# Memory attention: a slot's base as the bias of eight exponentials, and pauses in the written order

## The reference, cut to what matters

```python
q = _ln((x @ Wq.T + bq).reshape(-1, 48, 16), gq, bq_ln)
scores = jnp.einsum('bnd,nkd->bnk', q, key)              # 64 keys per slot
_, topi = jax.lax.top_k(flat, 8)
mask = jnp.ones_like(flat).at[..., topi].set(0.0)
sc = softmax(flat + -1000000.0 * mask)                   # over the eight kept
out = (einsum('bnk,nkd->bnd', sc, value) + q @ Wres.T + bres) @ Wmem.T + bmem
```

## Time and profile before

| | before |
|---|---|
| median of 3 runs | 4503.36 us (4493.08 to 4503.57) |
| profiled execution | 4485.82 us, span 4484.5 us |
| instructions | 52962 |
| TensorE busy, whole span | 3254.5 us (73%) |
| VectorE | 2467.1 us (55%) |
| ScalarE | 1627.5 us (36%) |
| GpSimd | 1403.0 us (31%) |
| memory attention | from the start to about 765 us |

### The profile page before, as it was taken

How to read it: one execution, slowest core, us unless ns; L and a number is a source line. 1 busy time by engine, 2 the same in 40 slices (tenths; PEclk the granted TensorE clock), 3 DMA queues, 4 the chain that set the end, 5 groups by cost and what they waited for, 6 DMA issues and landing times. The chain is left out here.

```text
span 4484.5 us, 52962 instructions
## 1 busy us (share of the span) xinstructions
PE 3254.5 (73%) x17693; PEld 2099.2 (47%) x17693; DVE 2467.1 (55%) x6511; ACT 1627.5 (36%) x3647; POOL 1403.0 (31%) x1086
## 2 busy tenths in 40 slices
PE   5988886868906666666888888467689567667698
PEld 3666665646602222223566656245456323235455
DVE  6878774364337788885323323545442277765443
ACT  3666653111205444542333333324212244434311
POOL 3666664104352434452212211200010244430010
PEclk7888888879958889898999999679769788889889
DMA  2000001203440000000000000110111200000000
GB/s 88 5 8 8 6 8 39 92 19 102 115 137 0 0 0 0 0 0 14 7 1 1 1 1 1 37 77 1 65 51 28 71 0 0 0 26 1 1 1 19
DMA packets 71034, 116.12 MB, mean 26 GB/s; under 512 B 28689, under 2 KB 58537, under 8 KB 68018
## 3 DMA queue, kind: packets, MB, share of 16 engines
q1 hardware_dynamic: 61170, 86.50, 5.7%
q0 software_dynamic: 9600, 26.23, 2.3%
HBM read 88.58 MB, written 24.12 MB: 25 GB/s over the span
## 5 line engine op out<-in xcount | busy, mean ns | idle before, releaser
L1223 POOL TENSOR_TENSOR L_attn_state<-L_attn_state,L_attn_ccol 128x1024 f32<-128x1024 f32 x192 | 451.7, 2353 | 589.3 <-DVE L_attn_state L1216 586.6
L1216 DVE TENSOR_TENSOR_SCAN L_attn_state<-L_attn_decay,bank 128x1024 f32<-128x1024 f32 x192 | 438.3, 2283 | 25.0 <-PE bank L1182 10.4
L1182 PE MATMUL bank<-L_attn_state,ident 128*128 128x512 f32 x768 | 408.1, 661 | 28.6 <-POOL L_attn_state L1223 28.6
L1176 PE MATMUL bank<-L_attn_parts,L_attn_select 96*128 96x512 bf16 x384 | 133.7, 432 | 257.5 <-DVE bank L1208 246.1
L1193 ACT ACTIVATE L_attn_decay<-L_attn_dt,L_attn_A 128x512 f32<-128x512 f32 x384 | 256.1, 715 | 142.9 <-DVE L_attn_state L1216 139.5
L1102 POOL TENSOR_TENSOR L_xattn_prob<-L_xattn_prob,L_xattn_inv 128x1024 f32<-128x1024 f32 x64 | 121.1, 1893 | 567.0 <-DVE L_xattn_inv L1085 567.0
L1208 DVE TENSOR_TENSOR bank<-L_attn_dtx,bank 128x1024 f32<-128x1024 f32 x192 | 235.9, 1229 | 72.2 <-PE bank L1176 66.4
L1182 PEld LDWEIGHTS bank<-L_attn_state,ident 128*128 128x128 f32 x768 | 161.2, 212 | 190.9 <-issue 122.8
L1198 ACT COPY L_attn_ccol<-bank 128x512 f32<-128x512 f32 x192 | 111.9, 583 | 309.3 <-PE bank L1176 186.8
L1176 PEld LDWEIGHTS bank<-L_attn_parts,L_attn_select 96*128 96x128 bf16 x384 | 28.8, 103 | 396.4 <-DVE bank L1208 355.8
L735 ACT ACTIVATE L_xattn_prob<-bank,L_xattn_top 128x128 f32<-128x128 f32 x512 | 135.4, 415 | 195.6 <-DVE L_xattn_top L777 195.6
(11 more groups left out here) (599 smaller groups left out, 7667.7 us busy)
## 6 DMA issues: line engine op xcount, KB each, us to landing
L_ffn_ew<-in_L_ffn_experts SPq DMA_DIRECT2D x4, 3072.0 KB, 21.1
L_ffn_made<-L_ffn_yout SPq DMA_DIRECT2D x24, 512.0 KB, 3.0
L_ffn_w<-in_L_ffn_w SPq DMA_DIRECT2D x4, 2048.0 KB, 14.7
L_xattn_ctx<-in_ctx_rows SPq DMA_DIRECT2D x3, 2048.0 KB, 8.5
L_ffn_rows<-L_ffn_xh SPq DMA_DIRECT2D x8, 512.0 KB, 2.9
L_ffn_made<-L_ffn_yout SPq DMA_DIRECT2D x12, 256.0 KB, 2.1
L_attn_rows<-in_x SPq DMA_DIRECT2D x16, 128.0 KB, 7.1
turned<-L_attn_rows SPq DMA_DIRECT2D x16, 128.0 KB, 2.3
```

What stands on the lines that cost most here:

```text
L1176: pe.matmul(self.spread.bank(2 * N + i)[:, :], self.select[:, NSTATE * i + n, :], parts[:, :], start=True, stop=True).then_inc(*self.sprea ...
L1182: t = pe.matmul(self.y[unit % len(self.y)][m][:, :], self.c.ident[:, :], self.state[N % 3][:, m, :], start=n == 0, stop=n == 15)
L1216: dve.tensor_tensor_scan(flat(self.state[N % 3]), flat(self.decay[N % 2]), flat(self.drive), 0.0, ALU.mult, ALU.add).then_inc(*self.scanne ...
L1223: pool.tensor_tensor(state[:, :, :], state[:, :, :], self.ccol[N % 2][:, :].unsqueeze(1).broadcast_to([P, 2, GT]), ALU.mult).then_inc(*sel ...
```

## The change

Three things are changed in `memory_attention`.

1. GpSimd's subtraction of the base (L2818) goes. ScalarE takes the exponential of a unit in eight instructions, one for each slot (both halves, 2 x 64 columns), with the slot's column of `base` as bias. For that, VectorE writes the negative base: -1 x best - logarithm, in one instruction.
2. In the order, `log` of unit n-1 stands ahead of `exp` of unit n-2, and `total` of unit n stands ahead of `spare` of n where it stood at the end of the iteration.
3. Steps `rest`, for which no engine has anything to do, are put in the lists: one in the front part ahead of the first `qturn`, and three ahead of the attend part. The steps behind them so come one place, and three places (one iteration), later. The front list then has 16 steps: `qturn`, `qcopy`, `qturn` of a sequence are the three of unit 4, and the last `qcopy` is issued ahead of the next sequence's first score. The attend list has 17: `pair`, `sm`, `pair` in unit 5, `sm`, `mix`, `den` in unit 0, `oT`, `mix`, `den` in unit 1, `oT`, `out`, `y` in unit 2, `ynorm` and `store` in unit 3.

```diff
@@ order()
         def front(a):
...
-                    ("scale", a), ("qmul", a), ("qturn", 2 * a), ("qcopy", 2 * a), ("qturn", 2 * a + 1), ("qcopy", 2 * a + 1)]
+                    ("scale", a), ("qmul", a), ("rest", a), ("qturn", 2 * a), ("qcopy", 2 * a), ("qturn", 2 * a + 1), ("qcopy", 2 * a + 1)]
         def attend(a):
-            return [("pair", 2 * a), ("sm", 2 * a), ("pair", 2 * a + 1), ("sm", 2 * a + 1), ...
+            return [("rest", a)] * 3 + [("pair", 2 * a), ("sm", 2 * a), ("pair", 2 * a + 1), ("sm", 2 * a + 1), ...
...
+            if 0 <= n - 1 < UNITS:
+                yield "log", n - 1
             if 0 <= n - 2 < UNITS:
                 yield "exp", n - 2
-            if 0 <= n - 1 < UNITS:
-                yield "log", n - 1
...
             if n < UNITS:
+                yield "total", n
                 yield "spare", n
...
-            if n < UNITS:
-                yield "total", n
@@ scalar()
         elif what == "exp":
-            both = t[n % RING][:, :, :, :].rearrange("p a s k -> p (a s k)")
-            act.wait_ge(*shifted.at(n))
-            act.activation(both, both, ACT.Exp).then_inc(*exped.up())
+            act.wait_ge(*spared.at(n))
+            act.wait_ge(*based.at(n))
+            for i in range(per):
+                both = t[n % RING][:, :, i, :]
+                m = act.activation(both, both, ACT.Exp, bias=base[n % 2][:, i:i + 1])
+            m.then_inc(*exped.up())
@@ vector()
         elif what == "base":
             if n >= 2:
-                dve.wait_ge(*shifted.at(n - 2))
+                dve.wait_ge(*exped.at(n - 2))
             dve.wait_ge(*logged.at(n))
-            dve.tensor_tensor(base[n % 2][:, :], top[n % 2][:, :, 0], tot[n % 2][:, :], ALU.add).then_inc(*based.up())
+            dve.scalar_tensor_tensor(base[n % 2][:, :], top[n % 2][:, :, 0], -1.0, tot[n % 2][:, :], ALU.mult, ALU.subtract).then_inc(*based.up())
@@ gpsimd()
-        elif what == "base":
-            pool.wait_ge(*spared.at(n))
-            pool.wait_ge(*based.at(n))
-            both = t[n % RING][:, :, :, :]
-            pool.tensor_tensor(both, both, base[n % 2][:, :].unsqueeze(1).unsqueeze(3).broadcast_to([P, 2, per, nkeys]), ALU.subtract).then_inc(*shifted.up())
```

More of the change, by code:

```diff
@@ L2375, in memory_attention @@
     scaled, topped, lowered, based, spared, totalled = (s.flag(k) for k in ("scaled", "topped", "lowered", "based", "spared", "totalled"))
-    raised, logged, exped, shifted, picked, positive = (s.flag(k) for k in ("raised", "logged", "exped", "shifted", "picked", "positive"))
+    raised, logged, exped, picked, positive = (s.flag(k) for k in ("raised", "logged", "exped", "picked", "positive"))
     negated, kept, inverted = (s.flag(k) for k in ("negated", "kept", "inverted"))
@@ L2386, in front @@
             return [("norm", a), ("xturn", a), ("xcopy", a), ("query", 2 * a), ("qadd", 2 * a), ("query", 2 * a + 1), ("qadd", 2 * a + 1), ("square", a), ("qsum", a),
-                    ("scale", a), ("qmul", a), ("qturn", 2 * a), ("qcopy", 2 * a), ("qturn", 2 * a + 1), ("qcopy", 2 * a + 1)]
+                    ("scale", a), ("qmul", a), ("rest", a), ("qturn", 2 * a), ("qcopy", 2 * a), ("qturn", 2 * a + 1), ("qcopy", 2 * a + 1)]
         def attend(a):
-            return [("pair", 2 * a), ("sm", 2 * a), ("pair", 2 * a + 1), ("sm", 2 * a + 1), ("mix", 2 * a), ("den", 2 * a), ("oT", 2 * a), ("mix", 2 * a + 1), ("den", 2 * a + 1),
+            return [("rest", a)] * 3 + [("pair", 2 * a), ("sm", 2 * a), ("pair", 2 * a + 1), ("sm", 2 * a + 1), ("mix", 2 * a), ("den", 2 * a), ("oT", 2 * a), ("mix", 2 * a + 1), ("den", 2 * a + 1),
                     ("oT", 2 * a + 1), ("out", a), ("y", a), ("ynorm", a), ("store", a)]
```

## The result

| | before | after |
|---|---|---|
| median of 17 runs each | 4501.16 us (4493.08 to 4505.68) | 4495.67 us (4489.29 to 4501.46) |
| ratio of the medians | | 0.9986 [0.998, 0.9993] |
| profiled execution | 4485.82 us, span 4484.5 | 4491.76 us, span 4490.5 |

The changed kernel is 5.5 us faster, less than the 0.3% that the prediction took as its bound for a difference. The gap that it forecast is there, but it ends 1.6 us later than worked out, and with that the saving inside a sequence is gone.

A forecast was written before the change was run, and what follows sets the result against it. TensorE, with its idle time and lowered clock, was taken as the bound. A sequence of 11.3 + 10.1 + 20.7 = 42.1 us against 43.0 saves 13.5 us over fifteen, plus 4 at the ends: 17.5, median 4486 us, range 4440 to 4515.

The forecast's parts named there:

- The gap that it forecast: TensorE at the second turn of queries, behind ScalarE's copy of the first: idle 4.1 us in one piece per sequence.
- Both waits: TensorE's 3.2 us for VectorE's product at the first turn and 2.0 us for GpSimd's addition at `pair`: both go.
- the likeliest case: Memory attention: one new gap, clock still falling; 42.1 us a sequence (41.3 to 43.9), kernel 4472 to 4513 us, chance 0.55.
- three signs of a wrong prediction: New wait under 3 us; mean clock over 0.93 or under 0.8; ScalarE over 85% busy with TensorE waiting for Relu copies.
- faster was put first: Whole kernel: chances given as faster 0.49, same 0.33, slower 0.18.
- the chain to the end of the gap: From the end of `out` through VectorE and ScalarE until `qcopy` frees the bank: 10.8 to 11.8 us, taken as 11.3.
- The other two pieces: Rest of a sequence after the gap: 10.1 us at 1.2 GHz, then 20.7 us at 2.4 GHz.
- eight exponentials: ScalarE, per unit: eight of 128 columns with bias replace one of 1.06 us and take 2.2 us.
- The clock staying up: Rival: TensorE stays at 2.4 GHz, some 3.5 us go, 38.6 us a sequence, kernel about 4435 us; chance 0.22.
- The clock coming back later: Rival: TensorE's low clock lasts longer than some 9 us; at 17 us, 45.7 a sequence, kernel 4540 us; chance 0.14.
- The wait only changes its place: Rival: exponentials of 3.3 us lengthen the gap by 1.1, old waits return, 43.2 us a sequence at least, 4500; chance 0.09.
- The 4 us that I counted at the stage's ends: Stage's ends: subtraction and exponential, 1.90 + 1.06 us, become 2.2 for some five units, saving 4 us.

The follow-up runs named there:

- the filled kernel: Changed kernel plus 24 transposes of the identity, which nothing reads, on TensorE ahead of the second turn of queries: 4462.58 us, ratio 0.9938 to before.
- One pause more: Changed kernel plus one more `rest` ahead of the second turn of the queries: 4459.27 us, ratio 0.9915 to before.
- `rcopy` first: Kernel with the later second turn, with ScalarE's Relu copies ahead of the eight exponentials in unit 4 of a sequence: 4434.21 us, ratio 0.9871 to before.

## Why the prediction came out as it did

**The mechanism was right.** Both waits went, one gap of 4.4 us (forecast 4.1) stands at the second turn of queries behind ScalarE's qT, the clock falls behind it (0.90 on average, forecast near 0.87), GpSimd is at 231 us (some 230), VectorE waits 1.6 us for `out`. 4495.67 us lies between 4440 and 4515, and within the likeliest case's own 4472 to 4513. None of the three signs of a wrong prediction is there. The range is 75 us wide for an effect of 5.5, so that the time lies in it says little; the wait, its place and the clock are what speaks for the prediction. The difference to the forecast is one of size: 0.14% where 0.4% was forecast, and so no difference where faster was put first.

**The mis-sized term is the chain to the end of the gap: 11.3 us forecast, 12.9 measured** (355.56 to 368.45). The other two pieces were right in sum, 10.1 + 20.7 forecast and 9.3 + 20.9 measured (to 377.74, then to 398.67), so this sequence is 43.1 us and not 42.1. Link by link from the end of `out`:

| end of | forecast | measured | why |
|---|---|---|---|
| sum of squares and scaling | 2.35 | 3.3 | the scaling of 48 columns took 1.29 us beside GpSimd's pick |
| eight maxima, difference | 3.9 | 5.2 | the difference took 0.80 instead of 0.3 |
| qmul | 5.4 to 6.2 | 7.3 | a wait of 0.33 for ScalarE's `qv`, and 1.22 instead of 0.94, beside GpSimd's work on y |
| eight exponentials | 7.9 to 8.7 | 10.0 | 2.43 instead of 2.2 |
| next difference | 8.8 to 10.3 | 11.4 | 1.33 beside the next pick |
| two Relu, an Exp, the top's exponential | 9.5 | 11.6 | |
| qcopy | 10.8 to 11.8 | 12.8 | |

Most of it is one thing: VectorE's scaling, first difference and product were held while GpSimd worked, by some 1.0, 0.4 and 0.2 us. The wait of 0.33 us for ScalarE, which no term of the sum had, and the exponentials' 0.1 to 0.2 are the rest, counted from the low end of the forecast, 10.8. The next difference was held longest, by 1.0 us, and cost next to nothing, since ScalarE's Exp ended at 11.4 as well. Scaling and product are held in every sequence, as the groups by line and form show (count | busy us, mean ns of one | idle before), first of after:

```profile
L2752 DVE TENSOR_TENSOR L_attn_q<-L_attn_q,L_attn_qv 128x768 f32<-128x768 f32 x14 | 17.4, 1246 | 5.0 <-ACT L_attn_qv L2606 5.0
L2749 DVE TENSOR_SCALAR L_attn_qv<-L_attn_qv 128x48 f32<-128x48 f32 x13 | 16.8, 1295 | 0.5
```

and of before, where the same two steps are L2749 and L2746:

```profile
L2749 DVE TENSOR_TENSOR L_attn_q<-L_attn_q,L_attn_qv 128x768 f32<-128x768 f32 x14 | 13.9, 994 | 1.8 <-ACT L_attn_qv L2606 1.8
...
L2746 DVE TENSOR_SCALAR L_attn_qv<-L_attn_qv 128x48 f32<-128x48 f32 x13 | 4.2, 327 | 0.5
```

The scaling alone is 0.97 us more than it was. The prediction had seen GpSimd hold VectorE and counted it only as an upper end, for the base and the second difference, and took the scaling from a sequence in which GpSimd held it little (0.32 us; without a GpSimd instruction beside it, it takes 0.19).

What brings scaling and pick together is not the exponentials, which had ended 1.3 us before that pick, at 356.35. GpSimd walks the written order too, and its short instructions for the norm of y (the last is L242) stand ahead of the pick and wait for VectorE's statistics of y, which wait for `out`. VectorE takes up the sum of squares and the scaling right behind those statistics, so the two meet in every sequence. They do so in every kernel with the pauses, which put `out` there, and in none without, whether the subtraction is kept or not. First the pauses alone, with the subtraction, then the exponentials alone, without it:

```profile
L2746 DVE TENSOR_SCALAR L_attn_qv<-L_attn_qv 128x48 f32<-128x48 f32 x13 | 16.8, 1290 | 0.5
```

```profile
L2750 DVE TENSOR_SCALAR L_attn_qv<-L_attn_qv 128x48 f32<-128x48 f32 x13 | 2.5, 189 | 0.5
```

So this part of the chain is a price of the new order. The next difference meets the pick that starts at the end of ScalarE's exponentials (at 365.61, behind 365.53).

The Trainium skill ("SBUF — State Buffer", Who interferes with whom) says that VectorE and GpSimd share a port pair, that a VectorE instruction contends for it if it has two inputs in SBUF or runs in a 2-port mode (which a `tensor_scalar` can), and that the one that starts first holds the pair for its whole instruction while the other is blocked. The rows agree: 357.66 + 1.29 = 358.95 and 357.64 + 1.27 = 358.91, and the eight maxima, with one input, took 1.10 us with a GpSimd instruction beside them and without.

**The exponentials** cost 2.43 us a unit, not 2.2. The row that I took, 2.17 us, reads PSUM. The group of all of them over the 600 us, 204.4 us for 84 units of eight:

```profile
L2628 ACT ACTIVATE L_attn_t<-L_attn_t,L_attn_base 128x128 f32<-128x128 f32 x672 | 204.4, 389 | 0.0
```

The estimate of 2.44 us from the Trainium skill ("ScalarE: Activation LUTs", What ACT_TABLE_LOAD costs) was right to 0.01.

**Small slips** of the working change nothing: its own terms give 8.6 to 10.1 for the next difference and not 8.8 to 10.3, and 44.05 us for the upper end of a sequence and not 43.9; and of the recall and score the 4.99 us run to the score's end, the 2.76 only to the next start, so that like with like (2.83) a microsecond costs 0.43 us.

**Not foreseen** was the wait of 0.98 us of a score for its bank: the score of unit 4 waits for `scopy`, which stands behind the same late top. It is a second piece of the same gap, so TensorE is idle for 1.0 + 4.4 + 0.95 us in this sequence in its three large waits, where 4.1 + 0.4 were forecast. That the clock comes back earlier than before was right: I had counted some 9 us at the lower level, and it is 6.9 in half of the sequences and 10.4 in the others.

**The rivals.** The clock staying up was wrong for this kernel. Its price was nearly right: 3.5 us a sequence were forecast, and the sequences of the filled kernel in which the clock stays up are 3.2 us shorter. One pause more brings most of it (0.94, ratio 0.9915). The clock coming back later was wrong: 10.5 us at most, where some 13.7 would have been needed. "The wait only changes its place", given 0.09, has the measured number, 43.2 us a sequence, but not its mechanism: the waits of the first turn and the pair did not come back (0.2 us and nothing), and the gap grew by longer steps on VectorE far more than by dearer exponentials.

**What the parts are worth.** No part alone gains: pauses 1.0022, exponentials 1.0037. The pauses alone exchange two waits for two others, as ScalarE's copies come late in each case. The exponentials alone lengthen ScalarE's queue in front of the short steps that q waits for. With the pauses they come to 1.0013, and the early logarithm and total then bring the 0.27% that make the whole a gain. A further pause and `rcopy` first take 1.15% more off. Whether these two need the lighter GpSimd isn't known: the kernel with the subtraction kept, a pause more and `rcopy` first was not run.

**What stays open.** The steady part got 0.2 us a sequence longer, some 3 us in all, and the medians 5.5 us shorter. The 4 us that I counted at the stage's ends don't show in the two profiles: VectorE's addition L448 at the start of the next stage begins at 778.40 us before and at 779.23 after. The rest of the kernel, which isn't changed, took 3706 us in the one and 3711 in the other, so single profiles differ by as much as the effect; the profiled execution of before was 15 us under its median, that of after 4 us. Where the 5.5 us lie isn't settled. That GpSimd holds VectorE in the chain was read from start and end times in the traces and from kernels that differ in more than that; a kernel with the pick elsewhere wasn't tried.

## What to carry to other kernels

A wait that is removed is worth only what the next one behind it leaves: before moving work, write down for each engine what its queue holds ahead of the step that will be late next, and try one further shift of that step, since here it was worth five times the change itself (0.71% against 0.14%). The pace of a loop is best read sequence by sequence: the mean clock promised 20 to 26 us that only three of twelve sequences had. A move between engines and a change of the order can each be worth less than nothing alone and pay only together, so test them together and apart. Where short VectorE steps are on the path, look at what GpSimd does at the same moment and not only at how busy it is.

## What the runs showed of the hardware

- A VectorE instruction of 48 columns took 0.19 us with no GpSimd instruction beside it, 0.33 us (mean) in the kernel before and 1.29 us when it started 0.02 us after a GpSimd instruction of 1.27 us; one of 768 columns took 0.94 us, 1.22 beside one and 2.53 beside another of GpSimd's.
- Eight exponentials of 128 columns with a bias took 2.43 us from SBUF and 2.17 us from PSUM.
- Transposes of the identity that nothing reads kept TensorE's clock up: 24 of them in 2.78 us raised the mean granted clock from 0.90 to 0.95 and made the kernel 22 us faster, 16 in 1.91 us from 0.94 to 0.98 and 23 us faster, both with up to 9 us of uncertainty.
- What time at 1.2 GHz costs depends on what else the sequence waits for. With the gap filled, 6.8 us at the lower level made a sequence 2.4 us longer (39.96 to 42.39). In the changed kernel four of six sequences with 10.4 us of it took the same 43.2 us as those with 6.9, and with `rcopy` first some 3 us of it the same 39.10 us as none.
